# Local attention on one core: VectorE adds the residual of the block before directly behind the scaling of the keys

## The chip, the cores and the metric

The program runs on one core of one Trainium2 chip. The metric is the device time of one execution in microseconds (us), median of the runs. TensorE (PE) does the matmuls and transposes, VectorE (DVE) the elementwise work and reductions, ScalarE (ACT) the exponentials, squares and copies out of PSUM, GpSimd (POOL) small elementwise work, and SyncE (SP) issues the DMAs. Each engine works through its own list of instructions in order; they meet only at semaphores.

## The reference, cut to what matters

The whole program is four blocks one after the other (a state-space layer, attention with experts, windowed attention, and a two-layer local-attention transformer), over an input of 16 x 256 tokens of 128 features. The change touches the attention half of the last block. For each of its two layers:

```python
h = shift_token(x)                       # second half of the features from the token before
q, k, v = split(h @ wqkv)                # 8 heads of 64
q, k = rotary_xpos(l2norm(q) * qs, l2norm(k) * ksc)
sim = where(mask, -max, 8 * q @ k.T)     # windows of 64 tokens, one window back
x = x + (softmax(sim) @ v) @ wo          # the residual addition
x = x + gated_feed_forward(x)
```

## The kernel before, in words

`phase_local` keeps the residual stream `R` (16 blocks of 2 x 128 tokens) in SBUF. For each layer n, `attend(n, b)` is called for the blocks b = 0 to 15, and each call makes two steps, c = 0 and c = 1, one for each half block of 128 tokens. Every engine has its own `attend`, written out by hand in the order in which that engine shall work. A step overlaps three stages: scores and softmax of half block (b, c), projection and rotary of the half block (b + 1, c), and output projection with residual of the half block (b - 1, c). All have VectorE work. Here "even step" is c = 0 and "odd step" is c = 1.

VectorE's step is, in order: `maxima` (L3058, row maxima of the scores in PSUM tile `s_ps`, then L3063, the bias `nbias` of the exponentials), `square_sums` of the queries (L3044), `rotary` of the next queries (L3031 to L3033, three products out of PSUM tile `qk_ps` into `c1` and `c2`), `scale_k` (L3050, keys times their inverse norm `rink`), `rotary` of the next keys (L3031 to L3033) and `rotary_sum` (L3038, `c1` plus `c2`), `residual` (L3078, `a_ps` plus `R`), `divide` (L3069 and L3072, probabilities over their sums, tile `pn`), and `square_sums` of the keys (L3044), which stands at the head of the next step's code.

TensorE's step is: `scores` (L2668, L2672 or L2678), in odd steps `transpose_r` (L2618), `transpose_p` (L2695), `project` of Q and K (L2630), `transpose_p`, `output` (L2732, into PSUM tile `a_ps`), `weigh` (L2715 or L2723), `turn_k` (L2655), `project_v` (L2635, again into `a_ps`), `weigh`, `turn_q` (L2645). Two of its waits matter here:

```python
pe.wait_ge(l.res_rd, NCH * (b - 1) + c + 1)   # in attend, ahead of project_v: a_ps is read
pe.wait_ge(l.sq_rd[Q], i + 1)                 # in turn_q: ScalarE has squared the queries
```

ScalarE's step is: in odd steps `shift` (L2874, L2875), `p_copy` (L2922), eight exponentials (L2913), `p_copy`, `k_copy` (L2902), `square` of Q and of K (L2881), `v_copy` (L2887), `o_copy` (L2928), `q_copy` (L2894). GpSimd's is: `rotary_sum` of the queries (L2558), `key_norms` (L2576, and the power L2579 into `rink`), `query_norms` (L2565, and the power L2569 into `qs`).

`residual` waits for `wo_mm`, which `output` of the same step counts up; the second product's semaphore `rot_rd` releases both `rotary_sum` and ScalarE's square. The first block's steps (`first=True`) have no residual, and the last block's (`last=2`) no rotary products. So a residual stands behind a rotary of the keys in the blocks b = 1 to 14: 28 steps in a layer, 56 in all.

Of the kernel before, what the change touches and what calls it, by code (L numbers as in the profile page):

```python
# [2419 lines left out]
def phase_local(nc, t, old, r_dram, x3_dram, out_dram):  # L2420
# [13 lines left out]
    with ExitStack() as ctx:  # L2434
# [59 lines left out]
        with nc.Block() as block:  # L2494
# [513 lines left out]
            def _(dve):  # L3008
# [10 lines left out]
                def rotary(n, b, c, x):  # L3019

                    l, i = at[n], NCH * b + c
                    dve.wait_ge(l.x_mm[x], i + 1)
                    at_least(dve, l.xT_mm[x], i - 1)
                    at_least(dve, l.sum_rd[x], i)
                    src = qk_ps[:, x, :].rearrange("p (h d) -> p h d", h=NH)

                    def table(k, d0, d1):
                        return t.tab[n][:, c, x, k, d0:d1].unsqueeze(1).to_broadcast([P, NH, d1 - d0])

                    hf = HD // 2  # L3030
                    dve.tensor_tensor(c1[x][c][:, :, :], src, table(0, 0, HD), ALU.mult)  # L3031
                    dve.tensor_tensor(c2[x][:, :, 0:hf], src[:, :, hf:HD], table(1, 0, hf), ALU.mult)
                    dve.tensor_tensor(c2[x][:, :, hf:HD], src[:, :, 0:hf], table(1, hf, HD), ALU.mult).then_inc(l.rot_rd[x], 1)  # L3033

                def rotary_sum(n, b, c, x):
                    l, i = at[n], NCH * b + c
                    dve.wait_ge(l.rot_rd[x], i + 1)
                    dve.tensor_tensor(c1[x][c][:, :, :], c1[x][c][:, :, :], c2[x][:, :, :], ALU.add).then_inc(l.sum_rd[x], 1)  # L3038

                def square_sums(n, b, c, x):  # L3040
                    l, i = at[n], NCH * b + c
                    dve.wait_ge(l.sq_rd[x], i + 1)
                    at_least(dve, l.sc_rd[x], i)
                    dve.tensor_reduce(ss[x][:, :], sq[x][:, :, :], AX.X, ALU.add).then_inc(l.ss_rd[x], 1)  # L3044

                def scale_k(n, b, c):
                    l, i = at[n], NCH * b + c
                    dve.wait_ge(l.rink_rd, i + 1)
                    dve.wait_ge(l.sum_rd[K], i + 1)
                    dve.tensor_tensor(c1[K][c][:, :, :], c1[K][c][:, :, :], rink[:, :].unsqueeze(2).to_broadcast([P, NH, HD]),  # L3050
                                      ALU.mult).then_inc(l.kn_rd, 1)

                def maxima(n, b, c):
                    l, i = at[n], NCH * b + c
                    dve.wait_ge(l.s_mm, i + 1)
                    dve.wait_ge(l.qs_rd, i + 1)
                    at_least(dve, l.nb_rd, i)
                    dve.tensor_reduce(top[:, :].rearrange("p (j r) -> p r j", r=2),  # L3058
                                      s_ps[:, :, :].rearrange("p r (j t) -> p r j t", j=NP), AX.X, ALU.max,
                                      negate=True).then_inc(l.top_s, 1)  # L3060
                    dve.wait_ge(l.top_s, i + 1)
                    at_least(dve, l.ex_rd, NH * i)
                    dve.tensor_tensor(nbias[:, :], top[:, :], qs[b % 2][:, c, :], ALU.mult).then_inc(l.nb_rd, 1)  # L3063

                def divide(n, b, c):
                    l, i = at[n], NCH * b + c
                    dve.wait_ge(l.ex_rd, NH * (i + 1))
                    at_least(dve, l.pn_rd, NU * i)
                    dve.reciprocal(ri[:, :], rs[:, :, :].rearrange("p u h -> p (u h)")).then_inc(l.ri_s, 1)  # L3069
                    dve.wait_ge(l.ri_s, i + 1)  # L3070
                    at_least(dve, l.pT_mm, NU * i)
                    dve.tensor_tensor(pn8[:, :, :], pe8[:, :, :], ri[:, :].unsqueeze(2).to_broadcast([P, NH, P]),  # L3072
                                      ALU.mult).then_inc(l.pn_rd, NU)

                def residual(n, b, c):
                    l = at[n]
                    dve.wait_ge(l.wo_mm, NCH * b + c + 1)
                    dve.tensor_tensor(R[:, b, c, :], a_ps[:, 0:C], R[:, b, c, :], ALU.add).then_inc(l.res_rd, 1)  # L3078

                def attend(n, b, first=False, last=0):  # L3080
                    for c in range(NCH):
                        summed = (b, 1) if c == 0 and not first else (b + 1, 0) if c == 1 and last < 2 else None
                        if summed:
                            square_sums(n, *summed, K)
                        maxima(n, b, c)
                        if summed:
                            square_sums(n, *summed, Q)
                        if last < 2:
                            rotary(n, b + 1, c, Q)
                        if c == 0:  # L3090
                            scale_k(n, b, 1)
                        elif last < 2:
                            scale_k(n, b + 1, 0)
                        else:
                            norm_stats(n, 0)
                        if last < 2:
                            rotary(n, b + 1, c, K)
                            rotary_sum(n, b + 1, c, K)
                        if not first:
                            residual(n, b - 1, c)  # L3100
                        divide(n, b, c)

                def norm_stats(n, g):
                    f, ln = ff[n], lns[n]
                    ln.turn(g)
                    dve.wait_ge(moved[g % 2], MOVES * (NG // 2 * n + g // 2 + 1))
                    for c in range(FC):
                        ln.mark(dve.bn_stats(stat[:, c, :], h[g % 2][:, c, :]))
                    ln.settle(apart=True)
                    for c in range(FC):  # L3110
                        ln.mark(dve.bn_aggr(mv[:, c, :], stat[:, c, :]))
                    ln.settle()
                    dve.tensor_scalar(ve[:, :], mv[:, :, 1], EPS, None, ALU.add).then_inc(f.var_rd, 1)
# [54 lines left out]
                for n in range(2):  # L3168
# [8 lines left out]
                    if n == 0:  # L3177
                        dve.wait_ge(cleared, CLEARED)
                    attend(n, 0, first=True)
                    for b in range(1, NB - 2):  # L3180
                        attend(n, b)
                    attend(n, NB - 2, last=1)
                    attend(n, NB - 1, last=2)
                    norm_apply(n, 0)
# [79 lines left out]
```

## Time and profile before

| what | value |
|---|---|
| median of 3 runs | 2167.82 us (2162.68 to 2170.45) |
| the profiled execution | 2166.1 us, of which its span 2164.3 us |
| busy share of the span | PE 80%, DVE 71%, ACT 57%, POOL 43% |
| TensorE's mean granted clock | 0.926 of full |
| attention steps with a residual, layer 0 | 1343.6 to 1624.1 us of the span |
| attention steps with a residual, layer 1 | 1750.4 to 2031.0 us of the span |

The times of the rows below are microseconds from the start of the span. A row of the timeline gives start, duration, engine, line, operation, the tiles written and read, and in brackets the idle time ahead of it with what ended it. Instructions of one kind that follow each other are merged ("x2"). The ends of matmuls are modelled.

### The profile page before, as it was taken

Reading aid. Unit: us, or ns where it says so; the run is one execution under the profiler, and the core shown is the slowest. Engines: PE = TensorE matmul, PEld = TensorE weight load, DVE = VectorE, ACT = ScalarE, POOL = GpSimd, SP = SyncE. Lnnn points to the kernel's source line nnn. Section 1 sums busy time; section 2 is a strip of 40 time slices with the busy share of each in tenths; the row PEclk is TensorE's granted clock in tenths of the full one; section 3 lists DMA queues with packets and bytes.
Section 4 is the critical chain, followed back from the end, with each engine's and each line's share of the span. In section 5 each row is a group of like instructions: output and inputs, shape, how many; then the busy total and the mean of one; then the engine's idle time right before and its main releaser. Section 6 shows DMA issues by size and latency. Waiting matters only on the chain. (4 is left out here: it accounts for less than half of the span.)

```text
span 2164.3 us, 38118 instructions
## 1 busy us (share of the span) xinstructions
PE 1727.5 (80%) x13216; PEld 960.0 (44%) x13216; DVE 1545.9 (71%) x3211; ACT 1232.1 (57%) x2673; POOL 931.7 (43%) x771
## 2 busy tenths in 40 slices
PE   5888988874898989859952756888888888888885
PEld 2333333332344444424422423555555555555553
DVE  5999999995677777722236666787875687787675
ACT  5778877741344444414434245887884388888721
POOL 5777887771012322223431134555541244555311
PEclk8999999996899999969985878999999999999997
DMA  4333333312111111114235141000001001000010
GB/s 149 113 108 123 118 107 114 101 49 61 55 39 37 39 39 40 31 35 134 66 94 185 33 132 35 21 16 16 16 12 24 16 11 25 16 11 16 15 42 22
DMA packets 107405, 125.56 MB, mean 58 GB/s; under 512 B 28804, under 2 KB 79151, under 8 KB 106224
## 3 DMA queue, kind: packets, MB, share of 16 engines
q1 hardware_dynamic: 103120, 115.07, 18.7%
q0 software_dynamic: 4096, 8.06, 1.1%
q8 instruction: 108, 1.77, 0.3%
q14 instruction: 81, 0.66, 0.1%
HBM read 71.60 MB, written 38.11 MB: 51 GB/s over the span
## 5 line engine op out<-in xcount | busy, mean ns | idle before, releaser
L394 POOL TENSOR_TENSOR m_bu<-m_dtu,m_brow 128x1024 f32<-128x1024 f32 x128 | 299.6, 2357 | 54.6 <-DVE m_hs L818 54.0
L818 DVE TENSOR_TENSOR_SCAN m_hs<-m_ps_da,m_bu 128x1024 f32<-128x1024 f32 x128 | 291.9, 2281 | 5.8 <-POOL m_bu L394 5.3
L1363 ACT ACTIVATE a_pt<-a_ps_s 128x1024 f32<-128x1024 f32 x128 | 131.0, 1024 | 226.3 <-PE a_ps_s L1141 226.3
L523 PE MATMUL m_ps_y_ps<-m_prod,m_ident 128*128 128x512 f32 x512 | 243.2, 597 | 0.0
L2913 ACT ACTIVATE l_pe<-l_ps_s,l_nbias,l_qs 128x128 f32<-128x128 f32 x512 | 226.5, 467 | 15.9 <-DVE l_nbias L3063 15.9
L1480 DVE TENSOR_REDUCE a_mpad<-a_ps_s 128x4 f32<-128x1024 f32 x128 | 156.8, 1225 | 92.0 <-PE a_ps_s L1133 90.9
L1133 PE MATMUL a_ps_s<-a_heads 32*128 32x256 f32 x1024 | 186.8, 445 | 43.8 <-DVE a_mpad L1480 29.0
L670 ACT ACTIVATE m_ps_da<-m_dt,m_a_neg 128x510 f32<-128x510 f32 x256 | 166.0, 681 | 72.6 <-DVE m_hs L818 72.0
L1141 PE MATMUL a_ps_s<-a_qm,a_heads 32*128 32x256 f32 x1024 | 184.8, 438 | 1.6 <-ACT a_pt L1363 1.2
L3058 DVE TENSOR_REDUCE l_top<-l_ps_s 128x8 f32<-128x1024 f32 x64 | 78.4, 1224 | 127.4 <-PE l_ps_s L2672 69.0
L1067 POOL TENSOR_TENSOR a_rstd<-a_ve,a_mhalf 128x2 f32<-128x2 f32 x48 | 33.8, 704 | 302.0 <-DVE a_ve L1438 162.5
L828 DVE TENSOR_TENSOR m_prod<-m_hs,m_ps_c_ps 128x1024 f32<-128x1024 f32 x128 | 153.2, 1197 | 12.2 <-PE m_ps_c_ps L509 12.2
L523 PEld LDWEIGHTS m_ps_y_ps<-m_prod,m_ident 128*128 128x128 f32 x512 | 96.6, 192 | 108.9 <-issue 106.9
L1133 PEld LDWEIGHTS a_ps_s<-a_heads 32*128 32x128 f32 x1024 | 82.0, 192 | 129.7 <-PE a_ps_s L1141 60.0
L2635 PE MATMUL l_ps_a<-t_wqkv,l_hT 128*128 128x512 f32 x128 | 72.8, 651 | 71.7 <-DVE t_r L3078 71.7
L2630 PE MATMUL l_ps_qk<-t_wqkv,l_hT 128*128 128x512 f32 x256 | 124.1, 607 | 0.8 <-ACT l_hT L2875 0.8
L509 PE MATMUL m_ps_c_ps<-m_bc,m_sel 96*128 96x512 bf16 x128 | 49.0, 383 | 78.3 <-DVE m_prod L828 67.7
L2913 ACT ACTIVATION_READ_ACCUMULATOR l_pe<-l_ps_s,l_nbias,l_qs 128x1 f32 x512 | 109.7, 214 | 0.0
L2569 POOL TENSOR_TENSOR l_qs<-l_sc,l_mhalf 128x8 f32<-128x8 f32 x64 | 106.6, 1666 | 5.4
L2579 POOL TENSOR_TENSOR l_rink<-l_sc,l_mhalf 128x8 f32<-128x8 f32 x64 | 106.6, 1666 | 5.3
L2922 ACT COPY l_pT<-l_ps_t 128x512 f32<-128x512 f32 x128 | 76.7, 600 | 54.8 <-PE l_ps_t L2695 54.1
L1760 POOL DMA_INDIRECT ys<-e_ys,e_back x64 | 62.2, 972 | 95.0 <-DVE e_back L1924 68.9
(344 smaller groups left out, 4143.0 us busy)
## 6 DMA issues: line engine op xcount, KB each, us to landing
m_brow<-state_rows SPq DMA_DIRECT2D x64, 512.0 KB, 4.3
slots<-m_void SPq DMA_DIRECT2D x16, 516.0 KB, 5.4
l_near<-l_v SPq DMA_DIRECT2D x64, 128.0 KB, 2.3
e_xs<-slots SPq DMA_DIRECT2D x16, 258.0 KB, 2.7
ys<-m_void SPq DMA_DIRECT2D x8, 512.0 KB, 5.4
qk<-a_qk SPq DMA_DIRECT2D x16, 256.0 KB, 2.0
a_heads<-qk SPq DMA_DIRECT2D x64, 64.0 KB
ew_w<-in_w SPq DMA_DIRECT2D x2, 2048.0 KB, 11.9
```

The lines of the kernel that those rows point to most:

```text
L394: nc.gpsimd.tensor_tensor(bu[s % 4][:, :, :], dtu[p][:, :, :], b2, ALU.mult).then_inc(bu_rd, 1)
L523: last = pe.matmul(y_ps[:, h, :], ident[:, :], prod[d % 3][:, h, :], start=False, stop=(s == NS - 1))
L670: last = nc.scalar.activation(da[s % 2][:, h, :, 1:], dt[p][:, h, :, 1:], ACT.Exp, scale=a_neg[:, h, s:s + 1])
L818: dve.tensor_tensor_scan(hs[s % 4][:, :, :].rearrange("p h t -> p (h t)"), da[s % 2][:, :, :, :].rearrange("p h q t -> p (h q t)"), bu[s % ...
L828: dve.tensor_tensor(prod[d % 3][:, :, :], hs[s % 4][:, :, :], c2, ALU.mult).then_inc(prod_rd, 1)
L1133: last = pe.matmul(dst[:, j, :], qT[p][r, g, c * P:(c + 1) * P], kT[p][r, g, :], start=True, stop=True)
L1141: last = pe.matmul(s2[:, j, :], kT[p][r, g, c * P:(c + 1) * P], qm[p][r, g, :], start=True, stop=True)
L1363: nc.scalar.activation(pt[t % 2][:, :, :], s2[:, :, :], ACT.Exp).then_inc(exp_rd, 1)
L1480: dve.tensor_reduce(dst, src[:, :, :], AX.X, ALU.max, negate=True).then_inc(max_rd, 1)
L2569: nc.gpsimd.tensor_tensor(qs[b % 2][:, c, :], sc[Q][:, :], mhalf[:, :], ALU.pow).then_inc(l.qs_rd, 1)
L2630: pe.matmul(qk_ps[:, x, :], hT[b % 2][:, c * P:(c + 1) * P], t.wqkv[n][:, x * INNER:(x + 1) * INNER], start=True, stop=True).then_inc(l.x_ ...
L2913: nc.scalar.activation(pe_[u % 2][:, h, :], s_ps[:, head % 2, j * P:(j + 1) * P], ACT.Exp, bias=nbias[:, head:head + 1], scale=qs[b % 2][: ...
```

## The change

`residual` moves up in VectorE's `attend`, from behind `rotary` and `rotary_sum` of the next keys to directly behind `scale_k`. Nothing else changes: the same instructions with the same operands and semaphores.

```diff
                         else:
                             norm_stats(n, 0)
+                        if not first:
+                            residual(n, b - 1, c)
                         if last < 2:
                             rotary(n, b + 1, c, K)
                             rotary_sum(n, b + 1, c, K)
-                        if not first:
-                            residual(n, b - 1, c)
                         divide(n, b, c)
```

## Rows read from the trace of the kernel before

**Rows 1.** Windows over the residual steps: us, busy time by engine, PE clock, DMA, GB/s.
```profile
1343.60:1624.10 280.50, 244.53 (x2267) 162.16 (x2268) 222.87 (x420) 229.66 (x698) 142.26 (x141) 1.00 0.08 17
1750.40:2031.00 280.60, 244.84 (x2270) 162.47 (x2270) 222.97 (x421) 229.64 (x698) 142.40 (x141) 1.00 0.08 17
```

**Rows 2.** Waits, 1100 to 2164 us: who for whom, us in total, times, longest.
```profile
PE l_ps_a L2635 <- DVE t_r L3078: 71.7, 56, 1.6
```

**Rows 3.** Timeline of VectorE, an even step from 1483.77 and an odd one from 1493.78.
```profile
1483.77 1.23 DVE L3058 TENSOR_REDUCE l_top<-l_ps_s 128x8 f32<-128x1024 f32 x1 [1.90 <-PE l_ps_s L2672]
...
1486.97 0.68 DVE L3050 TENSOR_TENSOR l_c<-l_c,l_rink 128x512 f32<-128x512 f32 x1
...
1488.95 0.71 DVE L3038 TENSOR_TENSOR l_c<-l_c 128x512 f32<-128x512 f32 x1
1489.59 0.28 DVE L3078 TENSOR_TENSOR t_r<-l_ps_a,t_r 128x128 f32<-128x128 f32 x1
...
1491.20 0.68 DVE L3044 TENSOR_REDUCE l_ss<-l_sq 128x8 f32<-128x512 f32 x1
1493.78 1.22 DVE L3058 TENSOR_REDUCE l_top<-l_ps_s 128x8 f32<-128x1024 f32 x1 [1.89 <-PE l_ps_s L2678]
...
1503.79 1.23 DVE L3058 TENSOR_REDUCE l_top<-l_ps_s 128x8 f32<-128x1024 f32 x1 [1.90 <-PE l_ps_s L2672]
```

**Rows 4.** Timeline of TensorE in the same two steps.
```profile
1486.30 1.06 PE L2732 MATMUL l_ps_a<-t_wo,l_oT 128*128 128x128 f32 x8
...
1487.90 0.66 PE L2655 MATMUL l_ps_t<-t_ident,l_c 128*128 128x128 f32 x4
1489.92 1.13 PE L2635 MATMUL l_ps_a<-t_wqkv,l_hT 128*128 128x512 f32 x2 [1.36 <-DVE t_r L3078]
...
1491.59 0.66 PE L2645 MATMUL l_ps_t<-t_ident,l_c 128*128 128x128 f32 x4
...
1496.51 1.06 PE L2732 MATMUL l_ps_a<-t_wo,l_oT 128*128 128x128 f32 x8
...
1498.08 0.66 PE L2655 MATMUL l_ps_t<-t_ident,l_c 128*128 128x128 f32 x4
1499.92 1.12 PE L2635 MATMUL l_ps_a<-t_wqkv,l_hT 128*128 128x512 f32 x2 [1.18 <-DVE t_r L3078]
...
1501.56 0.66 PE L2645 MATMUL l_ps_t<-t_ident,l_c 128*128 128x128 f32 x4
```

**Rows 5.** Timeline of ScalarE: the two squares of each of the two steps.
```profile
1489.67 1.14 ACT L2881 ACTIVATE l_sq<-l_ps_qk 128x512 f32<-128x512 f32 x2
...
1499.81 1.15 ACT L2881 ACTIVATE l_sq<-l_ps_qk 128x512 f32<-128x512 f32 x2
```

**Rows 6.** Timeline of GpSimd: the addition for the queries, even step.
```profile
1487.83 1.28 POOL L2558 TENSOR_TENSOR l_c<-l_c 128x512 f32<-128x512 f32 x1
```

**Rows 7.** Timeline of VectorE, the first block's odd step, which has no residual.
```profile
1334.63 1.22 DVE L3058 TENSOR_REDUCE l_top<-l_ps_s 128x8 f32<-128x1024 f32 x1 [0.65 <-PE l_ps_s L2678]
1335.88 0.17 DVE L3063 TENSOR_TENSOR l_nbias<-l_top,l_qs 128x8 f32<-128x8 f32 x1
...
1343.63 1.22 DVE L3058 TENSOR_REDUCE l_top<-l_ps_s 128x8 f32<-128x1024 f32 x1 [1.09 <-PE l_ps_s L2672]
```

**Rows 8.** Timeline of TensorE in that step.
```profile
1338.56 0.66 PE L2655 MATMUL l_ps_t<-t_ident,l_c 128*128 128x128 f32 x4 [0.45 <-DVE l_c L3050]
1339.06 1.02 PE L2635 MATMUL l_ps_a<-t_wqkv,l_hT 128*128 128x512 f32 x2
...
1341.43 0.63 PE L2645 MATMUL l_ps_t<-t_ident,l_c 128*128 128x128 f32 x4 [0.37 <-issue]
```

**Rows 9.** Timeline of ScalarE in that step.
```profile
1340.66 1.16 ACT L2881 ACTIVATE l_sq<-l_ps_qk 128x512 f32<-128x512 f32 x2
```

**Rows 10.** Timeline of GpSimd in that step.
```profile
1334.39 1.67 POOL L2579 TENSOR_TENSOR l_rink<-l_sc,l_mhalf 128x8 f32<-128x8 f32 x1
```

**Rows 11.** One line's instructions, 1340 to 2045 us: shortest, median, longest in ns.
```profile
L2881 ACT ACTIVATE l_sq<-l_ps_qk x122: 590/656/668, 1340.7 to 2027.0; 128x512 f32<-128x512 f32 x122
```

## The prediction

> **What bounds the kernel now.** The change reaches only the attention steps of the last block, so I read the windows over them first. In both layers TensorE is busy 244.5 to 244.8 of 280.5 us, VectorE 223, ScalarE 230, at a granted clock of 1.00 [rows 1]. No engine is full, so something makes them take turns. With 28 steps in each window a step is 10.02 us, and TensorE idles 36 us of the window, 1.28 us in a step.
>
> The list of waits names it: TensorE stands ahead of `project_v` (L2635) for the residual (L3078), 71.7 us in 56 waits, one in each step that the change touches [rows 2]. 71.7 / 56 is again 1.28 us, so this wait is all of TensorE's idle time there.
>
> The timelines say whether the wait costs time. I count from the start of the row maxima (L3058), called M. In the even step M is 1483.77, the residual runs from M+5.82 and ends at M+6.10, `project_v` begins at M+6.15 after 1.36 us of idling, `turn_q` at M+7.82, and the next maxima, released by the scores that follow `turn_q`, at M+10.01 [rows 3, 4]. VectorE itself had idled 1.89 us ahead of them. So each engine waits for the other once in a step, and the loop closes: maxima, VectorE's work up to the residual, `project_v`, `turn_q`, scores, maxima. Every 0.1 us taken out of that loop is 0.1 us of the step, until another wait ends last. The reader is to see two things: the wait of 1.28 us is on the path, and the residual is held by nothing but its place in VectorE's list.
>
> **What the change moves.** No instruction is added or removed, no DMA is issued earlier in SP's list, and no wait is new. The residual (0.28 us) changes places with three products and a sum.
>
> *The residual's new time.* `scale_k` starts at M+3.20 and takes 0.68, ending at M+3.88 [rows 3]. `output`, whose result the residual reads, ends at 1487.36, M+3.59, in the even step, and at 1497.57, M+3.79, in the odd one (M = 1493.78) [rows 4]. So it is there in both, in the odd step by 0.09 us. The residual would run from about M+3.85 to M+4.13, 1.97 us earlier than now.
>
> *TensorE at `project_v`.* `turn_k` starts at M+4.13 (even) and M+4.30 (odd) [rows 4], and in a step without residual `project_v` starts 0.50 us behind it [rows 8], so at M+4.63 and M+4.80. The residual is over 0.5 us before that: the wait is gone whole. By this alone TensorE gains 6.15 - 4.63 = 1.52 us in even steps and 6.14 - 4.80 = 1.34 in odd ones, 80 us over 28 of each. This is the upper bound.
>
> *What ends last next.* `turn_q` waits for ScalarE's square of the queries. ScalarE starts the two squares at M+5.90 in the even step and M+6.03 in the odd one [rows 5], at the end of a chain (exponentials, copies) that hangs on the maxima and not on the residual, so it stays put. TensorE would reach `turn_q` at 7.82 - 1.52 = M+6.30 (even) and 7.78 - 1.34 = M+6.44 (odd). One square takes 0.66 us [rows 11], so it is not done. GpSimd's addition for the queries, the other thing `turn_q` needs, ends at 1489.11, M+5.34 [rows 6], and is no limit.
>
> The trace has this case: the first block's odd step has no residual. There `turn_q` starts at 1341.43, 0.37 us late, and 0.77 us behind the start of the squares at 1340.66 [rows 8, 9]. The squares again start at M+6.03 (M = 1334.63), and the step lasts 9.00 us from maxima to maxima [rows 7], with the residual's step at 10.01 [rows 3]. So:
>
> - odd step: 10.01 - 9.00 = 1.01 us saved.
> - even step: `turn_q` at M+5.90+0.77 = M+6.67 for M+7.82 now, 1.15 us saved, a step of 8.86.
> - sum: 28 x 1.01 + 28 x 1.15 = 60.5 us.
>
> *What is pushed back.* The keys' products and sum come 0.2 us later (0.28 us less the overlap of starts). Their takers: ScalarE's square of the keys, which starts some 0.49 us behind the other (1.14 - 0.66), at M+6.39, while the products now end just before the sum's M+5.18, so at about M+5.4: covered by 1 us. The sum ends near M+6.1, and the division behind it starts where it does now, because residual plus products plus sum take as long in either order. VectorE ends its step with L3044 at 1491.88, M+8.11, against a next M at 8.86 or 9.00: 0.75 us to spare. Hence a residual that waits a few tenths for `output` costs nothing either. If that cover were gone, each 0.1 us would be 5.6 us.
>
> *Contention.* The residual now meets GpSimd's addition, which starts at M+4.06. The sum of the keys meets the addition's last 0.16 us today and takes 0.71 us, against 0.68 for `scale_k`, which meets nothing of it [rows 3, 6]: a few hundredths. I put the meeting at nothing, with 0.1 us a step as the other end, since 0.5 us of cover lies behind the residual. The shorter step also moves GpSimd's power for the keys beside the small product L3063 of the next step. In the first block it already is: the power runs 1334.39 to 1336.06 and L3063 at 1335.88 takes 0.17 us [rows 7, 10], not held. Nothing.
>
> The Trainium skill (SBUF — State Buffer, Who interferes with whom) says that a VectorE instruction with two SBUF inputs and a GpSimd instruction that reads SBUF exclude each other for the whole of the one that began first. By that rule L3063 would have been held to 1336.06, and the new odd steps would lose up to 0.1 us each, the sum being 58 instead of 60.5; this trace does not agree with it for this pair.
>
> *The clock.* TensorE gets fuller, not emptier, and these windows have a clock of 1.00 already [rows 1], so nothing comes from there.
>
> **The sum.** 2166.1 us for the profiled execution less 60.5 is 2105.6. The median of the runs shown is 1.7 us above that execution; I predict 2107 us.
>
> **The rivals.**
>
> *TensorE alone is the limit, 2088 us.* If the square were done by the time TensorE comes, all 80 us would come in. For it speaks that TensorE is the fullest engine; against it the 0.37 us of idling in the first block's step [rows 8].
>
> *Half of it given back, about 2133 us.* ScalarE is busy 8.2 us a step (229.66 / 28) [rows 1] of the 8.9 that would be left, so its last copies of one step come near the first of the next; if they run into it, exponentials and squares slip. With squares 0.5 us later in each step 28 us are lost, and about 33 of 60.5 us remain. Against it: 0.7 us a step are free, and the first block's step of 9.00 us has nearly all of that work [rows 7].
>
> *The wait only changes its name, 2166 us.* Had another release of `turn_q` or of the scores been due at the same time as now, nothing would move. The first block's step of 9.00 us [rows 7] speaks against it.
>
> *Slower: VectorE stands at the residual, 2183 us.* The place is the new residual, ahead of eight instructions of VectorE's list: three products, sum, reciprocal, division, sums of squares and the next maxima. It needs `output`, which TensorE does behind two projections and two transposes. VectorE's idle time is 1.9 us a step [rows 3], so the change turns into a loss when the residual waits more than 1.9 us, that is, when `output` ends later than M+5.8 instead of M+3.79. At 0.3 us beyond it 56 steps cost 17 us. The rows have `output` 2 us away from that point, and nothing that TensorE does ahead of it waits in the steady steps.
>
> The Trainium skill (Perfetto Trace Analysis, Tensor Engine Instruction) adds that a matmul's end in a profile is an estimate and its signal comes later, and that VectorE takes its instructions strictly in order. How much later no row here tells; by that rule the 0.09 us in hand in the odd step may be none, and the residual would stand for it.
>
> **How the numbers follow.** The squares as the limit: 0.75. TensorE alone: 0.06. Half given back: 0.12. No effect: 0.04. Slower: 0.03. The range leaves out the last two and most of the second and third. From the main case it takes the signal behind the square and the start of the squares, each uncertain by 0.1 us in 56 steps (11 us together), so 2096 to 2118 alone; towards the third case I stretch it to 2122. Faster by over 0.3% (6.5 us, about what a measurement of this kernel can tell from no change) is 0.93, within 0.3% 0.04, slower 0.03.
>
> **What would show it in the profile after.** Right: the wait of L2635 for L3078 is gone; the residual starts near M+3.85; L2645 has 0.3 to 0.4 us of idle time ahead of it in each step; steps of 8.86 and 9.00 us; both layers' 28 steps some 250 us instead of 280.5. Wrong: L2645 without idle time (then TensorE is the limit), squares later than M+6.0 (the third case), or idle time ahead of L3078 in tenths or more (the way to the slower case). The prediction fails if VectorE, now idle only 0.7 us in a step, or ScalarE, idle as little, sets the step by a wait that these rows do not show.

## The result and the profile after

| kernel | median of the runs, us | lowest to highest |
|---|---|---|
| before | 2168.89 (4 runs) | 2162.68 to 2170.45 |
| after | 2105.12 (4 runs) | 2104.13 to 2106.70 |

The kernel is faster: the ratio is 0.9712, with a 95% interval of 0.9698 to 0.9725, which is 63.8 us less. I had predicted 2107 us in a range of 2096 to 2122. The profiled execution of the kernel after took 2106.7 us, with a span of 2104.9.

The windows over the same 28 steps of each layer, and over what is left of the program, in the kernel after:

```profile
1342.80:1591.90 249.10, 239.01 (x2267) 161.43 (x2268) 222.60 (x421) 221.27 (x698) 141.28 (x141) 1.00 0.08 19
1719.40:1968.00 248.60, 238.51 (x2262) 161.06 (x2264) 222.51 (x420) 221.12 (x698) 140.80 (x140) 1.00 0.08 18
0.00:1342.80 1342.80, 1038.69 (x7545) 502.44 (x7546) 938.91 (x1894) 677.85 (x1066) 599.91 (x445) 0.90 0.28 82
1591.90:1719.40 127.50, 109.02 (x647) 71.04 (x647) 80.93 (x207) 58.58 (x136) 29.01 (x29) 0.92 0.08 17
1968.00:2104.90 136.90, 94.61 (x502) 63.90 (x500) 80.48 (x270) 36.70 (x76) 20.12 (x20) 0.84 0.12 29
```

Against [rows 1] the two windows are 31.4 and 32.0 us shorter, 63.4 us together, with nearly the same instructions in them. From maxima to maxima, 1342.83 to 1591.88 and 1719.44 to 1968.49, each layer's 28 steps take 249.05 us. TensorE, busy 87% before, is now busy 96%.

The three other windows hold 1607.2 us, and what lies outside the windows of [rows 1] is 2164.3 - 561.1 = 1603.2. So the spans differ by only 59.4 us. The other 4 us lie where the code is the same: 3.6 us behind the second layer (136.9 for 133.3, at a granted clock of 0.84 for 0.87) and 1.2 us between the layers, less 0.8 us ahead of the first. The four executions of the kernel before lie 7.8 us apart, so a single one can't settle 4 us; the medians have the 63.8.

The timelines of an even step (M = 1467.42) and an odd one (M = 1476.23) of the kernel after, VectorE first:

```profile
1467.42 1.22 DVE L3058 TENSOR_REDUCE l_top<-l_ps_s 128x8 f32<-128x1024 f32 x1 [0.87 <-PE l_ps_s L2672]
...
1470.63 0.68 DVE L3050 TENSOR_TENSOR l_c<-l_c,l_rink 128x512 f32<-128x512 f32 x1
1471.22 0.28 DVE L3078 TENSOR_TENSOR t_r<-l_ps_a,t_r 128x128 f32<-128x128 f32 x1
...
1476.23 1.22 DVE L3058 TENSOR_REDUCE l_top<-l_ps_s 128x8 f32<-128x1024 f32 x1 [0.72 <-PE l_ps_s L2678]
...
1480.06 0.29 DVE L3078 TENSOR_TENSOR t_r<-l_ps_a,t_r 128x128 f32<-128x128 f32 x1
...
1485.22 1.22 DVE L3058 TENSOR_REDUCE l_top<-l_ps_s 128x8 f32<-128x1024 f32 x1 [0.87 <-PE l_ps_s L2672]
```

TensorE in the same two steps:

```profile
1471.56 0.66 PE L2655 MATMUL l_ps_t<-t_ident,l_c 128*128 128x128 f32 x4
1472.05 1.02 PE L2635 MATMUL l_ps_a<-t_wqkv,l_hT 128*128 128x512 f32 x2
...
1474.07 0.63 PE L2645 MATMUL l_ps_t<-t_ident,l_c 128*128 128x128 f32 x4 [0.35 <-issue]
...
1481.03 1.02 PE L2635 MATMUL l_ps_a<-t_wqkv,l_hT 128*128 128x512 f32 x2
...
1483.03 0.63 PE L2645 MATMUL l_ps_t<-t_ident,l_c 128*128 128x128 f32 x4 [0.38 <-issue]
```

ScalarE's squares in them:

```profile
1473.32 1.15 ACT L2881 ACTIVATE l_sq<-l_ps_qk 128x512 f32<-128x512 f32 x2
...
1482.26 1.15 ACT L2881 ACTIVATE l_sq<-l_ps_qk 128x512 f32<-128x512 f32 x2
```

And the list of waits from 1100 us on, in which no row of L2635 waiting for L3078 is left:

```profile
PE l_ps_t L2645 <- issue: 22.8, 60, 1.3
```

The residual runs from M+3.80 and M+3.83 where it ran from M+5.82 [rows 3], and ends over 0.5 us before `project_v`, which follows `turn_k` by 0.49 us with no idle time between. In place of the 1.36 and 1.18 us ahead of `project_v` [rows 4] there are 0.35 and 0.38 us ahead of `turn_q`, 22.8 us in 60 waits, four of them in the first blocks. "Issue" says only that the profile names no releaser; the squares begin 0.75 and 0.77 us before `turn_q`, so that it starts just after the square of the queries is done.

### The profile page after: what moved, and what is told of

Read it like the earlier page. It is cut to its first block and busy times, and to the rows that moved or that the text cites. A ratio compares the mean times of both kernels' runs of the same rounds, so it can differ in the third digit from the quotient of the medians.

```text
span 2104.9 us, 38118 instructions
## 1 busy us (share of the span) xinstructions
PE 1719.8 (82%) x13216; PEld 959.9 (46%) x13216; DVE 1545.4 (73%) x3211; ACT 1215.5 (58%) x2673; POOL 931.1 (44%) x771
## 5 line engine op out<-in xcount | busy, mean ns | idle before, releaser
L2569 POOL TENSOR_TENSOR l_qs<-l_sc,l_mhalf 128x8 f32<-128x8 f32 x64 | 106.6, 1666 | 5.4
L2576 POOL TENSOR_SCALAR l_sc<-l_ss 128x8 f32<-128x8 f32 x64 | 15.4, 240 | 196.8 <-DVE l_ss L3044 196.8
```

The lines of the kernel that those rows point to most:

```text
L2569: nc.gpsimd.tensor_tensor(qs[b % 2][:, c, :], sc[Q][:, :], mhalf[:, :], ALU.pow).then_inc(l.qs_rd, 1)
```

## The experiments

Two theories about where the time comes from, and what holds the new kernel:

- **Loop.** TensorE and VectorE wait for each other once in a step, so the place of the residual in VectorE's list sets the step, one for one, until `turn_q`'s wait for the square ends last. In the kernel after, that wait is the limit.
- **Rivals.** The gain comes from something else in the new order (what the residual no longer runs beside, or the keys' products coming later); or another engine or TensorE alone holds the new kernel, so that the 0.36 us at `turn_q` are slack.

All ratios are to the kernel before on the same chip. The first four kernels below ran on a chip on which the kernel before took 2201.29 us; for the others it took 2168.86. A step is given from maxima to maxima, even and odd.

**Without the wait for the square, after.** The transposes of the first two half blocks (`kept[Q]` is 2) write the PSUM tile that the square reads, those of the later ones another, so the wait is kept for the first two alone.

```diff
                     pe.wait_ge(l.sum_rd[Q], i + 1)
-                    pe.wait_ge(l.sq_rd[Q], i + 1)
+                    if i < kept[Q]:
+                        pe.wait_ge(l.sq_rd[Q], i + 1)
```

> The changed kernel, with turn_q's wait for the square of the queries kept only for the first two half blocks of a layer, the ones whose transposes go into the bank that the square reads; later ones go into another bank. My theory (that wait is what ends last): TensorE starts turn_q when it comes to it, near M+6.30 and M+6.44 instead of M+6.64 and M+6.80, the 0.35 us of idling ahead of L2645 goes, and the time falls by some 0.36 x 56 = 20 us to about 2085 us. Rival (ScalarE or VectorE as a whole sets the step): the idling moves to another line of TensorE and the time stays near 2105 us.

Measured: ratio 0.9597 (0.9576 to 0.9618). A window of this kernel, and one step of VectorE (its lines stand one lower):

```profile
1400.00:1600.00 200.00, 200.00 (x1898) 135.54 (x1897) 187.07 (x351) 186.23 (x587) 118.49 (x119) 1.00 0.09 20
```
```profile
1486.94 1.23 DVE L3059 TENSOR_REDUCE l_top<-l_ps_s 128x8 f32<-128x1024 f32 x1 [0.32 <-PE l_ps_s L2679]
...
1495.52 1.23 DVE L3059 TENSOR_REDUCE l_top<-l_ps_s 128x8 f32<-128x1024 f32 x1 [0.45 <-PE l_ps_s L2673]
```

TensorE is busy for 200.00 of 200.00 us (the ends of matmuls being modelled), so there is no idle time left ahead of `turn_q` or anywhere, and a step is 8.58 us instead of 8.99. So the wait for the square was the limit of the kernel after, and TensorE's own row of work is the one behind it. The 28 steps of a layer take 237.85 us for 249.05, 22.4 us in both layers; the rest comes from the first blocks, whose steps waited for the square too.

**The same edit, before.** The same two lines in the kernel before.

> The kernel before with the same wait taken out and the residual left where it was. My theory: there the residual ends last and TensorE comes to turn_q at M+7.82, 1.15 us behind the square's release, so nothing changes: 2168 us, within 0.3%. Rival (the square also held the steps before the change): 5 to 20 us faster.

Measured: 0.9987 (0.9972 to 1.0002), no difference that the runs can tell. The row of the waits is that of [rows 2] again (its line is one lower):

```profile
PE l_ps_a L2635 <- DVE t_r L3079: 72.2, 56, 1.6
```

A wait that isn't last in its loop is worth nothing, and the same wait is worth over 1% once it is. This kernel shows both at once: its 56 steps with a residual are as long as before (280.72 and 280.49 us a layer for 280.51 and 280.29), while the two steps of layer 0's first block, which have no residual, take 7.44 and 8.50 us for 8.33 and 9.00.

**The residual halfway.** Behind the keys' products, ahead of their sum.

```diff
                         if last < 2:
                             rotary(n, b + 1, c, K)
-                            rotary_sum(n, b + 1, c, K)
                         if not first:
                             residual(n, b - 1, c)
+                        if last < 2:
+                            rotary_sum(n, b + 1, c, K)
```

> The kernel before with the residual moved half of the way, between the three products of the keys and their sum. My theory (each 0.1 us by which the residual comes sooner is 0.1 us of the step, until the square ends last): project_v starts near M+5.47 instead of M+6.15, still behind the place where TensorE would be ready, so 0.67 us a step are saved, 56 x 0.67 = 38 us, 2130 us. Rival (the residual only has to be ahead of the sum, or the order against the sum is what matters): the whole 63 us, 2105 us, or nothing, 2168 us.

Measured: 0.9798 (0.9780 to 0.9817), 2125 us by the chip of the result. VectorE and TensorE:

```profile
1479.49 1.23 DVE L3058 TENSOR_REDUCE l_top<-l_ps_s 128x8 f32<-128x1024 f32 x1 [1.29 <-PE l_ps_s L2678]
...
1484.56 0.28 DVE L3078 TENSOR_TENSOR t_r<-l_ps_a,t_r 128x128 f32<-128x128 f32 x1
...
1488.76 1.22 DVE L3058 TENSOR_REDUCE l_top<-l_ps_s 128x8 f32<-128x1024 f32 x1 [1.30 <-PE l_ps_s L2672]
```
```profile
1484.89 1.12 PE L2635 MATMUL l_ps_a<-t_wqkv,l_hT 128*128 128x512 f32 x2 [0.44 <-DVE t_r L3078]
...
1486.54 0.66 PE L2645 MATMUL l_ps_t<-t_ident,l_c 128*128 128x128 f32 x4
```

The residual stands at M+5.07, 0.75 us earlier than before, and the step is 9.27 us, 0.74 shorter than 10.01. `project_v` still waits and `turn_q` doesn't. This is the loop rule in its plain form: forecast 0.67 us a step, measured 0.74. The keys' products are still ahead of the residual here, so it isn't their coming later that pays; and the residual takes 0.28 us in its old, its middle and its new place, so it isn't what it runs beside either.

**The residual ahead of the scaling of the keys.** One place further up than the change.

```diff
                             rotary(n, b + 1, c, Q)
+                        if not first and last < 2:
+                            residual(n, b - 1, c)
                         if c == 0:
                             scale_k(n, b, 1)
...
-                        if not first:
+                        if not first and last == 2:
                             residual(n, b - 1, c)
                         divide(n, b, c)
```

> The residual one place further up than in the change, ahead of scale_k, in the 56 steps with rotary products. My theory: output's result is not there when VectorE comes at M+3.2, so VectorE stands 0.4 to 0.6 us at the residual until M+3.65 (even) and M+3.85 (odd); scale_k ends near M+4.53 and M+4.73, TensorE waits 0.45 us for it at turn_k and comes to turn_q some 0.1 us behind the square's release: 0.1 to 0.15 us a step, 7 us slower than the changed kernel, 2112 us. Rival (the residual's wait costs nothing, since project_v has cover): 2105 us. Rival (a standing VectorE drags the whole step): 0.5 us x 56 = 28 us, 2133 us.

Measured: 0.9713 (0.9692 to 0.9734), the same as the change, and not the loss that I had put on it. VectorE and TensorE:

```profile
1481.35 1.23 DVE L3058 TENSOR_REDUCE l_top<-l_ps_s 128x8 f32<-128x1024 f32 x1 [0.30 <-PE l_ps_s L2672]
...
1484.98 0.29 DVE L3078 TENSOR_TENSOR t_r<-l_ps_a,t_r 128x128 f32<-128x128 f32 x1 [0.34 <-PE l_ps_a L2732]
...
1490.17 1.22 DVE L3058 TENSOR_REDUCE l_top<-l_ps_s 128x8 f32<-128x1024 f32 x1 [0.29 <-PE l_ps_s L2678]
```
```profile
1483.88 1.06 PE L2732 MATMUL l_ps_a<-t_wo,l_oT 128*128 128x128 f32 x8
...
1485.92 0.66 PE L2655 MATMUL l_ps_t<-t_ident,l_c 128*128 128x128 f32 x4 [0.37 <-DVE l_c L3050]
...
1488.00 0.64 PE L2645 MATMUL l_ps_t<-t_ident,l_c 128*128 128x128 f32 x4
```

VectorE does stand 0.34 us for `output` (0.54 in the odd step), `scale_k` slips, and `turn_k` waits 0.37 us for it (0.40). But the idle time ahead of `turn_q` is gone instead, and `turn_q` stands at M+6.65 as in the kernel after. The wait has moved into the slack that the square leaves. My error was in two sizes: I had put 0.45 us at `turn_k`, and TensorE coming to `turn_q` at M+6.30, where without any wait it comes at M+6.23 (the kernel with the square first, below). So the slack is 0.42 us and the new wait fits in. The steps are 8.82 and 9.04 us for 8.81 and 8.99, 0.7 us a layer, which the ratio can't tell from nothing.

**The square of the queries first.** In the kernel after, ScalarE does it ahead of the copy of the transposed keys.

```diff
+                        if last < 2:
+                            square(n, b + 1, c, Q)
                         if c == 0:
                             k_copy(n, b, 1)
...
                         if last < 2:
-                            square(n, b + 1, c, Q)
                             square(n, b + 1, c, K)
```

> The changed kernel, with ScalarE's square of the queries moved ahead of its copy of the turned keys (k_copy); turn_q's wait for the square stays as it is. My theory (what ends last is when that square is done): the square starts 0.48 us sooner, at M+5.42 and M+5.56, its release at M+6.19 and M+6.33 comes before TensorE does (M+6.30 and M+6.44), so the 0.35 us of idling goes as it did without the wait: 20 us, a ratio to the kernel before of 0.961. Rival (k_copy, now 0.48 us later, is waited for by the transposes of the probabilities): part of it comes back there, a ratio of 0.965 to 0.971.

Measured: 2081.01 us, 0.9597 (0.9583 to 0.9611). TensorE:

```profile
1485.23 0.66 PE L2645 MATMUL l_ps_t<-t_ident,l_c 128*128 128x128 f32 x4
```

No idle time ahead of it, and steps of 8.42 and 8.58 us (M = 1479.00, 1487.42, 1496.00). The square earlier by one copy does the same as the square not waited for. This kernel changes nothing but an order and is 24 us below the change, with an interval that doesn't touch its own.

**Both edits of the square, after.** `turn_q` doesn't wait, and the square comes first.

> The changed kernel with both: turn_q's wait for the square only in the first two half blocks, and ScalarE's square of the queries ahead of k_copy. My theory (with either of them TensorE is full and sets the step, so the second has nothing left to give): a ratio of 0.960, as each alone. Rival (a square that is done sooner still shortens something): 0.957 or less.

Measured: 2080.34 us, 0.9586 (0.9571 to 0.9601), the same as either alone. A layer's 28 steps take 237.85 us with both, 237.85 without the wait and 237.96 with the square first. In its windows TensorE is again full:

```profile
1400.00:1580.00 180.00, 179.99 (x1723) 122.13 (x1722) 168.55 (x318) 167.72 (x529) 106.23 (x105) 1.00 0.08 18
```

**Spare work on VectorE, after.** One reduction of 128x512, whose result nobody reads, ahead of the residual, for its 0.60 us; then three of them.

```diff
+                        if last < 2:
+                            for _ in range(1):          # 3 in the second kernel
+                                dve.tensor_reduce(spare[:, _, :], wq, AX.X, ALU.max)
                         if not first:
                             residual(n, b - 1, c)
```

> The changed kernel with one more reduction on VectorE (128x512 out of SBUF into a spare tile, nobody's input) ahead of the residual in each step with rotary products; the output is the reference's. It costs VectorE 0.6 us a step and puts the residual, the keys' products, their sum and the division 0.6 us later. My theory (VectorE has 0.7 us to spare and the residual 0.5 us of cover): at most 0.1 us a step, a ratio of 0.971 to 0.974. Rival (VectorE sets the step by now, or the keys' products being late cost time): 0.6 us x 56 = 34 us, a ratio of 0.987.

> The same with three such reductions, 1.8 us a step. My theory: both covers are gone. VectorE's own step is 8.1 + 1.8 + some 0.1 = 10.0 us against 8.81 and 8.99, 1.1 us x 58 steps = 64 us, back to a ratio of 1.00. Rival (the residual alone matters, through project_v): it would start at M+5.65, release project_v at M+5.98, turn_q at M+7.65, and 0.9 us a step come back, a ratio of 0.995. Rival (no cover at all): 1.8 us x 56 = 101 us, a ratio of 1.018.

Measured: 0.9710 (0.9693 to 0.9727) with one, 0.9946 (0.9929 to 0.9964) with three. VectorE with one, then with three, and TensorE with three:

```profile
1478.97 1.23 DVE L3059 TENSOR_REDUCE l_top<-l_ps_s 128x8 f32<-128x1024 f32 x1
...
1487.97 1.22 DVE L3059 TENSOR_REDUCE l_top<-l_ps_s 128x8 f32<-128x1024 f32 x1 [0.31 <-PE l_ps_s L2673]
```
```profile
1480.89 1.22 DVE L3059 TENSOR_REDUCE l_top<-l_ps_s 128x8 f32<-128x1024 f32 x1
...
1484.69 1.86 DVE L3099 TENSOR_REDUCE l_spare<-t_wqkv 128x8 f32<-128x512 f32 x3
...
1490.68 1.21 DVE L3059 TENSOR_REDUCE l_top<-l_ps_s 128x8 f32<-128x1024 f32 x1
```
```profile
1486.81 1.13 PE L2636 MATMUL l_ps_a<-t_wqkv,l_hT 128*128 128x512 f32 x2 [1.12 <-DVE t_r L3079]
```

One is free: it uses up VectorE's idle time (0.72 to 0.87 us after) and the residual is still early enough. With three VectorE has no idle time at all and the step is 9.79 us, some 8.0 us of its own and three times 0.60; I had taken its own step at 8.2, and so a ratio of 1.00. The residual also holds `project_v` for 1.12 us again: it starts at M+5.58, 0.24 us earlier than before, and the step is 0.22 us shorter than before, as the loop alone would have it. The rival that went by `project_v` alone had 0.995 and met the time. So VectorE's fullness and the loop give the same step here within hundredths. The time can't tell them apart, and only the missing idle time says that VectorE is full.

**The residual behind the division, before.** The same loop, longer: in the kernel before, for the steps with rotary products.

```diff
-                        if not first:
+                        if not first and last == 2:
                             residual(n, b - 1, c)
                         divide(n, b, c)
+                        if not first and last < 2:
+                            residual(n, b - 1, c)
```

> The kernel before with the residual moved the other way, behind the division, in the 56 steps with rotary products. My theory (the residual's place is the step's length): it starts 1.45 us later, at M+7.27, and each step is 1.45 us longer: 81 us, a ratio of 1.037. Rival (the wait at project_v is a place where slack collects, not the limit): less than half of that, a ratio under 1.02.

Measured: 2308.32 us, 1.0642 (1.0624 to 1.0660), 139 us lost where I had 81. VectorE, windows over the wait and the 4.20 us behind it, and TensorE:

```profile
1470.59 1.23 DVE L3058 TENSOR_REDUCE l_top<-l_ps_s 128x8 f32<-128x1024 f32 x1 [4.91 <-PE l_ps_s L2672]
...
1482.02 1.23 DVE L3058 TENSOR_REDUCE l_top<-l_ps_s 128x8 f32<-128x1024 f32 x1 [3.32 <-PE l_ps_s L2678]
...
1495.04 1.23 DVE L3058 TENSOR_REDUCE l_top<-l_ps_s 128x8 f32<-128x1024 f32 x1 [4.91 <-PE l_ps_s L2672]
```
```profile
1486.30:1489.60 3.30, 0.69 (x7) 0.43 (x5) 3.17 (x8) 2.91 (x9) 1.06 (x1) 1.00 0.00 0
1489.60:1493.80 4.20, 3.98 (x15) 2.01 (x16) 0.53 (x1) 1.73 (x3) 1.91 (x2) 0.59 0.21 46
```
```profile
1489.59 1.51 PE L2635 MATMUL l_ps_a<-t_wqkv,l_hT 128*128 128x512 f32 x2 [2.61 <-DVE t_r L3078]
...
1492.09 1.12 PE L2645 MATMUL l_ps_t<-t_ident,l_c 128*128 128x128 f32 x4
```

The short step, 11.43 us, is the theory's: 10.01 and the 1.42 us by which the residual comes later. The long one is 13.02 us. In it TensorE stood 2.61 us at `project_v`, and in the 4.20 us after that its granted clock was 0.59, most of it at the lower level of 1.2 GHz; the four transposes of `turn_q` take 1.12 us instead of 0.66. Of the 56 steps 37 are long, and in each of the 37, and in no other, the transposes of `turn_q` take the longer time. So 56 x 1.42 = 80 us come from the loop, and 37 times 1.56 us, 58 us, from the clock: 138, against 139 by the ratio.

**One spare reduction, before.** Behind the keys' sum and ahead of the residual, to lengthen the loop by less.

```diff
                             rotary_sum(n, b + 1, c, K)
+                            if not first:
+                                dve.tensor_reduce(spare[:, 0, :], wq, AX.X, ALU.max)
                         if not first:
                             residual(n, b - 1, c)
```

> The kernel before with one spare reduction on VectorE ahead of the residual, in the 56 steps; the output is the reference's. The residual comes 0.6 us later, TensorE idles 1.9 us a step at project_v. My theory (the residual's start sets the step, one for one, and the further loss of the run with the residual behind the division came from a lower TensorE clock after its waits of 2.6 to 2.8 us): 0.6 x 56 = 34 us, a ratio of 1.0155, at a clock of 1.00 in these steps. Rival (the clock falls after waits of 1.9 us too): longer matmuls behind project_v in some steps and a ratio over 1.025. Rival (a spare reduction costs nothing here, as it did in the changed kernel): a ratio of 1.00.

Measured: 2223.17 us, 1.0240 (1.0219 to 1.0262). VectorE, and TensorE:

```profile
1455.12 1.23 DVE L3059 TENSOR_REDUCE l_top<-l_ps_s 128x8 f32<-128x1024 f32 x1 [1.90 <-PE l_ps_s L2673]
1467.30 1.23 DVE L3059 TENSOR_REDUCE l_top<-l_ps_s 128x8 f32<-128x1024 f32 x1 [3.47 <-PE l_ps_s L2679]
1477.90 1.23 DVE L3059 TENSOR_REDUCE l_top<-l_ps_s 128x8 f32<-128x1024 f32 x1 [1.90 <-PE l_ps_s L2673]
```
```profile
1461.86 1.13 PE L2636 MATMUL l_ps_a<-t_wqkv,l_hT 128*128 128x512 f32 x2 [1.94 <-DVE t_r L3079]
1463.56 1.12 PE L2646 MATMUL l_ps_t<-t_ident,l_c 128*128 128x128 f32 x4
```

Most steps are 10.60 us, 0.59 more than 10.01, one for one again. Twelve of the 56, six in each layer, are 12.10 to 12.35 us, such as the one from 1455.12 to 1467.30, and the transposes behind the wait take 1.12 us in them. 56 x 0.59 = 33 us, and 12 x 1.57 = 19 us, are the 52 us that the ratio gives. The loop's part was as forecast; the ratio of 1.0155 was missed because the clock falls here too, which was the rival's mechanism (its number was over 1.025).

## Why the prediction was right

- *The wait is on the path.* Shown from both sides. The residual later by 0.59 us makes the step longer by 0.59, later by 1.42 longer by 1.42, and earlier by 0.75 shorter by 0.74.
- *The residual's new time.* Forecast M+3.85, measured M+3.80 and M+3.83, with no idle time ahead of it. The 0.09 us in hand in the odd step weren't all there. In the experiment ahead of `scale_k` the waiting residual starts 0.04 us behind the modelled end of `output` (1483.88 + 1.06 = 1484.94, and 1484.98). In the odd step of the kernel after, `output` ends at 1478.96 + 1.06 = 1480.02 and the residual starts at 1480.06, the same 0.04 us behind it, and 0.03 us later behind `scale_k`'s start than in the even step. The Trainium skill (Perfetto Trace Analysis, Tensor Engine Instruction) says that the signal comes later than the estimated end; these rows agree, with 0.04 us. It cost nothing: VectorE may stand there 0.34 us for nothing, as that experiment shows. That answers the slower rival.
- *The wait goes whole, 1.52 and 1.34 us.* `project_v` was forecast at M+4.63 and M+4.80, and stands at M+4.63 and M+4.80.
- *The square ends last next.* Forecast M+6.67 and M+6.80 for `turn_q`, with 0.3 to 0.4 us of idle time; measured M+6.65 and M+6.80, with 0.35 and 0.38. Taking the wait away or doing the square earlier makes the step shorter at once, which shows it. The rival "TensorE alone" gave 2088 us: it was one wait too early. With that wait gone the kernel takes 2081, so its 80 us were too small as well. `turn_q` comes 1.67 and 1.64 us behind `project_v` where that had waited [rows 4], and 1.61 and 1.57 us behind it in the kernel with the square first (M+6.23 for the forecast 6.30), and the first blocks' steps gain too.
- *Steps of 8.86 and 9.00 us.* Measured 8.81 and 8.99. The first block's odd step had given the odd one to 0.01 us, and rightly so: with the square's wait taken out of the kernel before, that step shrinks to 8.50 us, so it had the same limit. The even one, for which there was no such row, I made 0.05 us too long: `turn_q` came 0.02 us sooner and the maxima 0.03 sooner behind it.
- *The pushed-back work.* The squares stood at M+5.90 and M+6.03, where they had been, and VectorE idles 0.87 and 0.72 us for the forecast 0.75. The spare reduction, 0.60 us, fitted into that. So "half of it given back" had no footing: ScalarE's last copy of the even step starts at 1475.22 and its first work of the next at 1476.57, with 0.66 us of idle time ahead of it. (That rival's "about 2133" leaves out the 1.7 us between the profiled execution and the median, which 2107 and 2088 have; its sum gives 2135.)
- *Contention.* Put at nothing, and so it was: `scale_k` and the products behind the residual take 0.68 us as before. For the pair of the Trainium skill's rule (SBUF — State Buffer, Who interferes with whom) the rows of the kernel without the square's wait are the sharpest for L3063, GpSimd and then VectorE:

```profile
1487.03 1.67 POOL L2579 TENSOR_TENSOR l_rink<-l_sc,l_mhalf 128x8 f32<-128x8 f32 x1
```
```profile
1488.20 0.17 DVE L3064 TENSOR_TENSOR l_nbias<-l_top,l_qs 128x8 f32<-128x8 f32 x1
```

L3063 (L3064 there) starts 0.50 us before the power is over, ends 0.33 us before it, and takes its usual 0.17 us. By the rule it would have been held until 1488.70. The kernel after has a wider case: `scale_k`, 128x512 with two SBUF inputs, runs from 1479.43 to 1480.11 in its usual 0.68 us, wholly inside the power L2569, 1478.67 to 1480.34. By the rule it would have begun 0.91 us later. The profile's spans on GpSimd are rough, so the edges of such overlaps are uncertain by an amount that no row gives; as far as the rows go, the measurement decides, and these pairs don't exclude each other.

- *The sum.* 60.5 us forecast, 62.7 us in the two layers' steps (280.5 + 280.3 - 2 x 249.05), 63.8 us between the medians. Of the missing 2.2 us the even steps' 0.05 us are 1.4. The last such step of each layer, 8.85 and 8.84 us, gives 0.3, and one step of the kernel before that took 10.25 us 0.2; the rest is hundredths.

## What to carry to other kernels

Two engines that wait for each other once in a step make a loop, and the step is as long as the loop: moving the released instruction in its in-order list moves the step one for one, and work elsewhere in the step costs nothing as long as it stays inside the idle time. How far the gain goes is set by the wait that ends last next, and a neighbouring step of the same trace that lacks the dependence (here the first block's) gives it to hundredths. Then look at that wait at once: 0.36 us ahead of `turn_q`, 22.8 us in all, were worth 24 us more for one swap in ScalarE's order, while the same wait taken out of the kernel before was worth nothing in its 56 steps.

## What the runs showed of the hardware

Lengthening a wait of TensorE cost more than the wait. With 1.18 and 1.36 us at `project_v` the granted clock was 1.00 over both windows [rows 1, 4]. With 1.78 to 2.19 us it fell in 12 of 56 steps, with 2.6 to 3.0 us in 37 of 56. Each fall brought some matmuls to the level of 1.2 GHz and about 1.6 us to the step. The wait's length in one step doesn't decide it; in the kernel with one spare reduction ahead of the late residual:

```profile
1571.22 1.12 PE L2636 MATMUL l_ps_a<-t_wqkv,l_hT 128*128 128x512 f32 x2 [1.95 <-DVE t_r L3079]
1573.04 1.12 PE L2646 MATMUL l_ps_t<-t_ident,l_c 128*128 128x128 f32 x4
...
1594.00 1.13 PE L2636 MATMUL l_ps_a<-t_wqkv,l_hT 128*128 128x512 f32 x2 [1.94 <-DVE t_r L3079]
1595.67 0.66 PE L2646 MATMUL l_ps_t<-t_ident,l_c 128*128 128x128 f32 x4
```

The same wait and the same work ahead of it, and the clock falls behind the one and not behind the other. Whether the single wait or TensorE's lower busy share brings it about was not separated.
